# The C.B products of a chunk computed without their masked quarter: narrower matmuls in a Mamba-2 block on one core

## What is computed

```python
H, P, N, G = 128, 64, 128, 8      # heads, head width, state size, groups
CHUNK = 128                       # so each sequence is 2 chunks
L = exp(segsum(A_dt))             # lower triangle: zero for s > l
Y_diag = einsum('bzlhn,bzshn,bhzls,bzshp->bzlhp', C, B, L, xch)
```

## Time and profile before

| | |
|---|---|
| median of 3 runs | 1727.06 us (1726.54 to 1727.39) |
| profiled execution, its own time | 1727.64 us |
| its span on the core | 1725.5 us |
| TensorE busy | 1698.0 us, 98% of the span |
| VectorE, ScalarE, GpSimd busy | 1259.4, 843.2, 1202.5 us |
| mean granted TensorE clock | 0.998 |
| `cbs`, lines 984 to 986 | 12 products, eight times; 64 records to a line |

### The profile page before, as it was taken

One profiled execution on the slowest core, in us unless ns is written; L12 is line 12 of the kernel. 1 busy time (PEld: TensorE's weight loads), 2 busy tenths in 40 slices (PEclk: granted clock), 3 DMA queues, 4 the chain that ended last, 5 costly groups with the idle time before them and its releaser, 6 DMA issues.

```text
span 1725.5 us, 38927 instructions
## 1 busy us (share of the span) xinstructions
PE 1698.0 (98%) x12596; PEld 1392.2 (81%) x12596; DVE 1259.4 (73%) x1894; ACT 843.2 (49%) x1275; POOL 1202.5 (70%) x872
## 2 busy tenths in 40 slices
PE   6999999999999999999999999999999999999998
PEld 5788888888888888888888888888888887788887
DVE  7888548863887289728883788468845887877777
ACT  4666346643664366536653665356634663222221
POOL 4599659964997489757985799569955988433330
PEclk9999999999999999999999999999999999999999
DMA  3332013301231123103220222023201311111101
GB/s 103 100 93 87 19 50 93 93 25 49 75 93 43 31 81 93 55 19 86 84 71 19 74 84 83 19 62 88 87 11 57 93 56 64 50 37 50 49 13 49
DMA packets 71341, 107.23 MB, mean 62 GB/s; under 512 B 16740, under 2 KB 25060, under 8 KB 71304
## 3 DMA queue, kind: packets, MB, share of 16 engines
q1 hardware_dynamic: 70296, 105.38, 20.5%
q10 hardware_dynamic: 1008, 1.38, 0.3%
HBM read 103.51 MB, written 3.15 MB: 62 GB/s over the span
## 4 chain that ended last, share of the span: by engine, by line
PE 95%; DVE 2%; ACT 1%; POOL 1%; issue 1%; DMA 1%; SPq 0%; ACTq 0%; POOLq 0%; DVEq 0%
PE proj L893 18%; PE proj L895 17%; PE proj L894 17%; PE y L1061 9%; PE y L1034 6%; PE y L1036 6%; PE y L1035 6%; PE y L1048 3%; PE y L893 2%; PE y L895 2%; PE y L894 2%; PE decay L1008 1%; PE decay L894 1%; PE decay L893 1%; PE decay L895 1%; PE decay L1183 1%
## 5 line engine op out<-in xcount | busy, mean ns | idle before, releaser
L893 PE MATMUL proj<-xhi,w_hi 128*128 128x512 f32 x1072 | 433.1, 404 | 0.3 <-issue 0.3
L895 PE MATMUL proj<-xhi,w_lo 128*128 128x512 f32 x1072 | 419.6, 391 | 0.0
L894 PE MATMUL proj<-xlo,w_hi 128*128 128x512 f32 x1072 | 418.4, 390 | 0.0
L516 POOL TENSOR_TENSOR g_lo<-gated,g_hi 128x512 fp32r<-128x512 f32 x127 | 162.2, 1279 | 184.2 <-ACT g_hi L768 184.2
L1251 DVE SCALAR_TENSOR_TENSOR v<-proj,par_sb,v 128x510 f32<-128x510 f32 x378 | 275.2, 742 | 20.8 <-DVE v L1251 9.7
L893 PEld LDWEIGHTS proj<-xhi,w_hi 128*128 128x128 f32 x1072 | 201.6, 188 | 57.7 <-issue 14.9
L895 PEld LDWEIGHTS proj<-xhi,w_lo 128*128 128x128 f32 x1072 | 201.5, 188 | 44.1
L894 PEld LDWEIGHTS proj<-xlo,w_hi 128*128 128x128 f32 x1072 | 202.1, 189 | 37.5
L534 POOL TENSOR_TENSOR gated<-hs,gate 128x512 f32 (+1 forms) x126 | 188.6, 1518 | 47.9 <-DVE hs L1386 47.9
L477 POOL TENSOR_TENSOR w_lo<-w_raw,w_hi 128x512 fp32r<-128x512 f32 x144 | 182.6, 1288 | 55.5 <-ACT w_hi L643 55.3
L662 ACT ACTIVATE v<-proj,par_sb 128x512 f32<-128x512 f32 x126 | 98.1, 778 | 237.1 <-PE proj L895 237.1
(11 more groups left out here) (202 smaller groups left out, 3272.8 us busy)
## 6 DMA issues: line engine op xcount, KB each, us to landing
w_raw<-in_win SPq DMA_DIRECT2D x144, 256.0 KB, 2.7
fade_l<-faded SPq DMA_DIRECT2D x128, 256.0 KB, 3.3
wo_raw<-in_wout SPq DMA_DIRECT2D x64, 256.0 KB, 2.6
M<-in_w SPq DMA_DIRECT2D x14, 512.0 KB, 3.8
row_r<-rows SPq DMA_DIRECT2D x256, 3.0 KB
row_l<-rows SPq DMA_DIRECT2D x256, 3.0 KB
cb<-in_w SPq DMA_DIRECT2D x7, 512.0 KB, 3.3
out<-resid SPq DMA_DIRECT2D x8, 256.0 KB, 2.0
```

The lines of the kernel that those rows point to most:

```text
L516: e.tensor_tensor(g_lo[:, i % 2, :, :], tokens(t, kk), g_hi[:, i % 2, :, :].bitcast(F32), ALU.subtract)\
L893: e.matmul(o, hi_l, hi_r, start=first, stop=False)
L894: e.matmul(o, hi_l, lo_r, start=False, stop=False)
L895: return e.matmul(o, lo_l, hi_r, start=False, stop=last)
```

## The change

Only `cbs` changes. `past` is computed as before. Of the two masked products of each sequence, the half of l that can take from all s is computed from all 128 rows (stationary 128 columns, moving 64 columns): the second half of l for sequences 0 and 1 and, these being reversed, the first half for 2 and 3, as `(high, low)[b // 2]`. The other half of l is computed from its own 64 s alone (stationary 64 columns, moving 64 columns), in a second loop, in which a product into partitions 0 to 63 (`low`) alternates with one into partitions 64 to 127 (`high`). The block of 64 s by 64 l that the mask takes out is no longer written; VectorE's operations are as before. So 12 products become 20.

```diff
                 for b in range(B):
-                    first, second = 2 * b * P, (2 * b + 1) * P
-                    cols = slice(b * P, (b + 1) * P)
-                    e.matmul(first_own[:, cols], bc[:, 0, first:first + P], bc[:, 1, first:first + P], start=True, stop=True)
-                    e.matmul(past[:, cols], bc[:, 0, first:first + P], bc[:, 1, second:second + P], start=True, stop=True)
-                    mm = e.matmul(misc[:, cols], bc[:, 0, second:second + P], bc[:, 1, second:second + P], start=True, stop=True)
+                    product(past, b, 0, whole, 1, whole)
+                    product(first_own, b, 0, whole, 0, (high, low)[b // 2])
+                    product(misc, b, 1, whole, 1, (high, low)[b // 2])
+                for b in range(B // 2):
+                    for z, o in ((0, first_own), (1, misc)):
+                        product(o, b, z, low, z, low)
+                        mm = product(o, b + B // 2, z, high, z, high)
                 mm.then_inc(cbr.sem, 1)
```

More of the change, by code:

```diff
@@ L980, in cbs @@
                 pe.wait_ge(silu.sem, nsilu)
-                for b in range(B):
-                    first, second = 2 * b * P, (2 * b + 1) * P
-                    cols = slice(b * P, (b + 1) * P)
-                    e.matmul(first_own[:, cols], bc[:, 0, first:first + P], bc[:, 1, first:first + P], start=True, stop=True)
-                    e.matmul(past[:, cols], bc[:, 0, first:first + P], bc[:, 1, second:second + P], start=True, stop=True)
-                    mm = e.matmul(misc[:, cols], bc[:, 0, second:second + P], bc[:, 1, second:second + P], start=True, stop=True)
+                def product(o, b, s_chunk, s_part, l_chunk, l_part):
+                    s_first, l_first = (2 * b + s_chunk) * P + s_part[0], (2 * b + l_chunk) * P + l_part[0]
+                    return e.matmul(o[s_part[0]:s_part[0] + s_part[1], b * P + l_part[0]:b * P + l_part[0] + l_part[1]],
+                                    bc[:, 0, s_first:s_first + s_part[1]], bc[:, 1, l_first:l_first + l_part[1]],
+                                    start=True, stop=True)
+                whole, low, high = (0, P), (0, HD), (HD, HD)
+                for b in range(B):
+                    product(past, b, 0, whole, 1, whole)
[5 more added lines that the diff above has]
+                        mm = product(o, b + B // 2, z, high, z, high)
                 mm.then_inc(cbr.sem, 1)
```

## The result

The changed kernel takes 1733.36 us (median of 6 runs, 1732.36 to 1734.65) against 1727.22 us (6 runs, 1726.54 to 1728.29): a ratio of 1.0034, 95% interval [1.0024, 1.0044]. The forecast was 1732.5 us. The profiled execution took 1732.36 us.

A forecast was written before the change was run, and what follows sets the result against it. TensorE was taken as the bound. Seven windows at +0.70 us (+4.9 us) and the first call (+0.5 us) gave +5.4 us on the profiled 1727.64 us, 0.58 us over the median: forecast 1732.5 us, range 1730.0 to 1735.0 us.

The forecast's parts named there:

- TensorE is the bound and the change goes in one to one: Seven of eight `cbs` lie where TensorE never waits (66 to 1420 us), so their growth adds fully to the time.
- A half product costs as much as a whole one: In `cbs`, 128-column loads set the pace: 0.110 us a record against 0.111, saving 0.02 us a window.
- The run of quarters, 0.72 us a window: In each window's `cbs`, eight new pairs (some 0.45 us) plus draining and uncovered loads add 0.72 us.
- The first call, +0.5 us: Ahead of the first tile, TensorE waits for VectorE's chain released by the first `cbs`, so `exponents` comes 0.5 us later.
- The price of a half-clock stretch, 1.6 us: Rival, chance 0.09: a TensorE half-clock stretch, costing 1.6 us, goes or a third comes: 1730.9 or 1734.1 us.
- (a): Expected in the changed profile, a window's `cbs`: half records start 0.110 us apart, not 0.058.
- (c): Expected in a window: 0.7 us more from the last record before `cbs` to the eleventh block's first weights.
- (d): Expected in the changed profile: TensorE still without a wait from 66 to 1420 us.
- (e): Expected in the changed profile: the first `exponents` 0.5 us later.
- (b): Expected in `cbs`: 16 narrow records in some 0.65 us, a gap before, and an idle load entry of about 0.2 us or more.
- half products at their stream's pace: Rival, chance 0.08 (at or near that pace): `cbs` half products follow their 64-column stream, 0.058 us a record: 1726.2 us.
- pairs one after another: Rival, chance 0.04: quarter pairs in `cbs` do not run side by side, +0.47 us in each of eight calls: 1736.2 us.

The follow-up runs named there:

- the cut by l: Kernel before, with each masked square computed whole as two products of 128 stationary and 64 moving columns, no quarters: 1740.68 us, ratio 1.0078.
- two cuts by s: Kernel before, masked squares as products of 64 stationary and 128 moving columns, nothing skipped: 1729.83 us; or triangle only, such products plus 64 by 64 quarters: 1726.68 us.
- the order without pairs: Changed kernel with four quarter products into partitions 0 to 63, then four into 64 to 127, not alternating: 1735.18 us, ratio 1.0047.

## Why the prediction was right, and where it was off

1. *TensorE is the bound and the change goes in one to one*: right. No wait from 66 to 1420 us, and the lateness grows there in seven equal steps and hardly anywhere else.
2. *A half product costs as much as a whole one*: right, and it was the step that decided. The load pace that `variances` and line 1061 gave, and the load alone of the earlier trace rows, are what the cut by l confirms.
3. *The run of quarters, 0.72 us a window*: right in kind, 5% low. Less the 0.02 us for the half products the sum had 0.70 us; it measured 0.76. Three terms were each 0.02 us too small: the pairs took 0.47 us where the 0.72 had 0.45 for them, the turn 0.29 us where it had 0.27, and the 0.02 us saved by the half products did not come, since their loads stand 0.1117 us apart and not 0.110. Seven windows: 5.3 us, not 4.9.
4. *The first call, +0.5 us*: wrong, 0.06 us. The failed step is "`exponents` follows on its last link at 59.74": the named releaser was taken at its word. The row loads ended the wait, with 1.2 us of slack. Even the 0.06 us is no price of the change: in the five kernels with the row loads in their old place where they end the wait and the products of the first call are altered, the way to `exponents` is 0.08 us shorter to 0.42 us longer than before, in no order of their windows.
5. *The price of a half-clock stretch, 1.6 us*: wrong for the second one, and the profile after shows it without an experiment. The wait of about 3 us ahead of it was there again, but the granted clock stayed at its upper level:

```profile
1481.50:1484.90 3.40, 0.77 (x5) 0.38 (x4) 3.29 (x9) 0.38 (x1) 2.33 (x2) 1.00 0.00 0
1484.90:1488.30 3.40, 3.26 (x15) 2.40 (x14) 3.23 (x10) 1.71 (x3) 1.91 (x1) 1.00 0.42 154
```

   Yet the lateness against the kernel before is 4.73 us ahead of this place and 4.74 behind. VectorE is busy 3.2 to 3.3 of 3.4 us here, at either clock, and TensorE, which makes up 1.2 us, waits these 1.2 us longer a little later, ahead of the same matmul, in the kernel before and in the changed one:

```profile
1489.73 0.47 PE L893 MATMUL y<-wo_hi,g_hi 128*128 128x512 f32 x1 [0.36 <-issue]
```

```profile
1494.46 0.47 PE L893 MATMUL y<-wo_hi,g_hi 128*128 128x512 f32 x1 [1.56 <-issue]
```

   The stretch was priced from its matmuls alone, without asking who is late next. The starts of VectorE's operations answer that in part: from 1470 to 1500 us every one of them is 4.73 to 4.75 us later than in the kernel before, also where TensorE has caught up to 3.5. The two cuts by s have no second stretch either, and there too the lateness is the same ahead of the place and behind it. That it is VectorE which ends this wait is argued from these rows; no run took it away.
6. *The sum*: +5.4 us forecast, +6.1 us measured, on paper 5.3 + 0.1. That the paper sum is again 5.4 is luck: the windows were 0.4 us too low and the first call 0.4 us too high. What is left, 0.7 us, is within the spread of the runs (2.3 us for the changed kernel, 1.8 for the one before) and the interval of the ratio, 4.1 to 7.6 us; the profiled pair differs by 4.7 us, of which -0.8 us lies ahead of the first `cbs`. No further cause is needed, and none was looked for.
7. *What would show each step*: (a), (c) and (d) came as said, (a) by the loads, 0.111 us apart, while the matmul records start 0.058 to 0.165 us apart; (e) did not. Of (b) the length came (0.69 us against 0.65; the working given for it, 7 x 0.058 + 0.22, makes 0.63), but the idle "issue" entry for the weight loads of `cbs` did not: the modelled end of the last wide load, 0.192 us long, covers all but 0.07 us of the gap. The entry was expected as it stands for line 1129, where the wide matmul ahead streams 512 columns.

The rivals: half products at their stream's pace are refuted by the cut by l, pairs one after another by the order without pairs and by the 0.69 us of the run. On the latter, the Trainium skill ("TensorE: Matmul & The Clock Gate", section "Part 3: Packing small matmuls — row/col tiling") has a rule that a load overlaps with matmuls in flight only in another row group. It is at odds with these runs: the changed kernel's quarters all use the 128 rows, and their 16 loads and matmuls fit into 0.69 us. The same section also lets a load go ahead into the background weight buffer; no run here can tell whether that is what these loads do.

## What to carry to other kernels

When a triangle or a mask lets a matmul be smaller, make the stationary side smaller, or leave it whole: under 128 stationary columns a float32 product of 64 moving columns took exactly as long as one of 128, so the cut has to shorten the load as well as the stream. A run of narrow products also pays once for turning there and back (0.29 us here behind 64 moving columns, 0.35 us behind 128), so a skipped quarter has to be worth more than that, and the runs should be gathered, not spread. And a wait for several semaphores is to be checked against the end of the operation named as its releaser: one that ends after the wait did cannot have released it.

## What was not expected of the hardware

- Four products to one half of the array's columns, followed by four to the other half, overlap in part: 16 records took 0.97 us, where pairs took 0.69 us and strict sequence would have taken about 1.15 us.
- A matmul's own start is no longer an even clock when loads set the pace. In the changed kernel the matmul records of wide products start 0.058, 0.112 or 0.165 us apart and carry lengths from 222 to 328 ns, presumably since a short stream ends before the next weights are there; the loads stay 0.111 us apart. Loads, not matmul starts, are to be read in such a stretch.
- A stretch at half clock (10 matmuls in 3.4 us) could go without any change of the time: TensorE made up 1.2 us and then waited 1.2 us longer. Another such stretch moved by 9 us, when the first call was done twice, and cost 1.5 us there.
